# A two-layer decoder whose last mixture scatters its finished rows to the output and fetches its expert weights tile by tile

## The reference, cut to what matters

```
x = x + attn(LN(x)); x = x + xattn(LN(x), ctx); x = x + moe0(LN(x))        # layer 0: stages A, B, C
x = x + relattn(LN(x)); x = x + xattn(LN(x), ctx)                          # layer 1: stages D, E
h = x + attention(rms(x, g1));  out = h + moe1(rms(h, g2))                 # stages F, G

moe1(xf):                                                  # xf: 2048 tokens x 128
  vals, idx = top_k(xf @ router_w + router_b, 2);  scores = softmax(vals)
  emask = one_hot(idx) * (pos < cap);  tmask = sum(emask, -1);  m = max(assign, -1)
  y = (gelu((xf @ w2[m]) * (xf @ w1[m])) @ w3[m])          # one expert of 8 for each token, hidden 256
  out = sum_k scores[k] * (y if tmask[k] > 0 else xf)
```

## Time and profile before

| | us |
|---|---|
| median of 3 runs | 1674.38 |
| lowest, highest run | 1672.79, 1678.52 |
| profiled execution | 1675.38 |
| its span, first to last instruction | 1673.6 |
| mean granted TensorE clock (share of full) | 0.922 |

### The profile page before, as it was taken

One profiled execution on the slowest core, in us unless ns is written; L12 is line 12 of the kernel. 1 busy time (PEld: TensorE's weight loads), 2 busy tenths in 40 slices (PEclk: granted clock), 3 DMA queues, 4 the chain that ended last, 5 costly groups with the idle time before them and its releaser, 6 DMA issues.

```text
span 1673.6 us, 43831 instructions
## 1 busy us (share of the span) xinstructions
PE 1423.6 (85%) x17681; PEld 878.2 (52%) x17681; DVE 966.6 (58%) x2541; ACT 749.0 (45%) x1927; POOL 232.3 (14%) x201
## 2 busy tenths in 40 slices
PE   4889888696499999999958999889989898999672
PEld 3343434393266666766633466346644564456462
DVE  4354635323477777777723676576665776477532
ACT  1323142251266666666613276327723672447431
POOL 1011120123030030200010200030002100120124
PEclk7989999797799999999978899999989998899897
DMA  9600000023230100100021000000000000000012
GB/s 327 264 17 1 17 1 7 17 58 98 77 140 4 26 19 10 35 4 16 4 76 43 1 2 2 5 7 2 2 5 7 2 2 1 7 1 1 6 55 70
DMA packets 62072, 60.07 MB, mean 36 GB/s; under 512 B 27952, under 2 KB 47024, under 8 KB 60720
## 3 DMA queue, kind: packets, MB, share of 16 engines
q1 hardware_dynamic: 59536, 53.04, 10.0%
q0 software_dynamic: 2048, 4.20, 0.9%
q10 hardware_dynamic: 288, 0.03, 0.0%
HBM read 32.73 MB, written 24.51 MB: 34 GB/s over the span
## 4 chain that ended last, share of the span: by engine, by line
PE 69%; DVE 15%; issue 4%; SPq 4%; DMA 3%; ACT 3%; POOL 2%; ACTq 0%; POOLq 0%; DVEq 0%
PE ps L1126 7%; PE ps L1514 6%; PE ps L1533 5%; PE ps L500 5%; PE ps L1547 4%; PE ps L1106 4%; PE ps L1116 4%; DVE arena L586 4%; PE ps L1147 4%; PE ps L258 4%; PE ps L1502 3%; PE ps L474 3%; PE ps L1161 2%; PE ps L1556 2%; PE ps L797 2%
## 5 line engine op out<-in xcount | busy, mean ns | idle before, releaser
L1259 DVE TENSOR_REDUCE nmax<-ps 128x1 f32<-128x512 f32 x256 | 166.8, 683 | 56.3 <-PE ps L1116 55.7
L1590 ACT ACTIVATE arena<-ps,arena 128x512 f32<-128x512 f32 (+3 forms) x256 | 135.5, 531 | 119.1 <-DVE arena L1650 112.9
L1650 DVE TENSOR_REDUCE arena<-ps 128x1 f32<-128x512 f32 (+3 forms) x256 | 124.3, 487 | 78.8 <-PE ps L1518 76.7
L1219 ACT ACTIVATE arena<-ps,nmax 128x512 f32<-128x512 f32 x172 | 119.0, 692 | 80.8 <-DVE nmax L1259 79.3
L1533 PE MATMUL ps<-sqc,arena 128*128 128x128 f32 x640 | 106.6, 287 | 20.0 <-DVE arena L1658 19.7
L586 DVE TENSOR_REDUCE arena<-ps 128x8 f32<-128x1232 f32 x64 | 89.2, 1438 | 40.3 <-PE ps L462 40.1
L258 PE MATMUL ps<-identb 128*128 128x512 bf16 x408 | 110.0, 430 | 1.4 <-DVE kcol L707 1.4
L1267 DVE COPY arena<-ps 128x512 f32<-128x512 f32 x128 | 88.0, 688 | 39.9 <-PE ps L1126 38.4
L1514 PE MATMUL ps<-arena 64*128 64x384 f32 (+3 forms) x512 | 106.2, 493 | 0.0
L1658 DVE TENSOR_SCALAR arena<-arena 128x512 f32<-128x512 f32 (+3 forms) x256 | 100.8, 394 | 9.1
L598 DVE RECIPROCAL arena<-ps 128x128 f32<-128x128 f32 x8 | 7.7, 959 | 160.4 <-PE ps L500 160.4
(11 more groups left out here) (350 smaller groups left out, 2713.1 us busy)
## 6 DMA issues: line engine op xcount, KB each, us to landing
xs_d<-onehot SPq DMA_DIRECT2D x3, 3072.0 KB, 29.6
cw<-in_cw SPq DMA_DIRECT2D x2, 2048.0 KB, 13.4
rv<-in_rv SPq DMA_DIRECT2D x2, 1536.0 KB, 19.7
late<-in_gw SPq DMA_DIRECT2D x3, 1024.0 KB, 10.8
arena<-xs_d SPq DMA_DIRECT2D x46, 64.0 KB, 1.8
xs_d<-arena SPq DMA_DIRECT2D x46, 64.0 KB, 1.6
xs_d<-onehot SPq DMA_DIRECT2D x1, 2560.0 KB, 22.4
onehot<-q_s SPq DMA_DIRECT2D x96, 8.0 KB
```

What stands on the lines that cost most here:

```text
L1219: nc.scalar.activation(PB[k % 6], ps[:, k % 5, :], ACT.Exp, bias=nmax[:, u:u + 1], accum_out=rsum[:, b % 2, u:u + 1]).then_inc(SD["exp"], 1)
L1259: nc.vector.tensor_reduce(nmax[:, k % NU:k % NU + 1], ps[:, k % 5, :], AX.X, ALU.max, negate=True)\
L1590: nc.scalar.activation(TF["p%d" % (n % 2)][:, h * S:h * S + wd], ps[:, FSB[n % 2][h], 0:wd], ACT.Exp, bias=TF["nmax"][:, k4:k4 + 1], accum ...
L1650: nc.vector.tensor_reduce(TF["nmax"][:, k4:k4 + 1], ps[:, FSB[n % 2][h], 0:wd], AX.X, ALU.max, negate=True)\
```

## The change: what it does, and the diff

1. **Rows.** For G there is a new DRAM table `gs_d` of 23,552 rows of 258 floats (1032 bytes). A row holds the normed token, its residual, its weight `cy` and its token number less 4096. They lie in SBUF as `G4`, in the space of stage C's weights (`cw`). GpSimd scatters whole rows of it.
2. **Clearing.** `gs_d` is cleared by four DMAs of GpSimd (`pool_G_zero`), placed between `pool_C` and `pool_D`. The old `xs_d` and its clearing by SyncE stay, for stage C.
3. **Result.** VectorE's last step of a tile multiplies by the row's `cy` and adds the row's residual. GpSimd then scatters the 128 finished rows to `out`; rows with an index out of bounds (the cleared ones) are left out. The store to the table, the gather of 16 times 128 rows, the 16 adds and the output stores are gone.
4. **Weights.** w1 and w2 of G are no longer resident (group 4 loses two loads of 1 MB), and GpSimd doesn't copy them. SyncE reads the expert's number and issues two loads from DRAM per tile, into four buffers.
5. **Masks.** The eight mask steps, and the two copies of `cpick` and `cmask`, go from VectorE to GpSimd (`pool_prepare`), before GpSimd's first work for stage B. VectorE keeps the two small steps for `pcol`, now after the norm of stage B.
6. Three small VectorE instructions that write the token numbers, before D1.

```diff
+        def pool_prepare(pool):
+            pool.wait_ge(s_const[1], 16 * len(GROUPS[1]))
+            nc.gpsimd.tensor_copy(xmask[:, :, 0:KP], xmask_in)
+            nc.gpsimd.tensor_copy(xmask[:, :, KP:KW], xmask_in[:, :, 0:KW - KP])
+            for mask, given in ((amask, amask_in), (kmask, kmask_in)):
+                nc.gpsimd.memset(mask[:, :, KS:KP], MASKED)
+                nc.gpsimd.tensor_scalar(mask[:, :, 0:KS], given[:, :, :], MASKED, None, ALU.mult)
+                ins = nc.gpsimd.tensor_scalar(mask[:, :, KP:KW], given[:, :, 0:KW - KP], MASKED, None, ALU.mult)
+            ins.then_inc(s_mask, 1)
+            nc.gpsimd.tensor_copy(cpick[:, :, :], causal_in[:, 0:2, :])
+            nc.gpsimd.tensor_copy(cmask[:, :, :], causal_in[:, 2:4, :]).then_inc(s_mask, 1)
...
         def pool_G_send(pool, b):
             pool.wait_ge(SG["slot"], b + 1)
-            for n in range(NT):
-                nc.gpsimd.indirect_dma_start(xs_d, bass.IndirectOffsetOnAxis(ap=slot4[:, b * NT + n:b * NT + n + 1], axis=0),
-                                             yn4(b)[:, n, :], None).then_inc(SC["sent"], 16)
+            if b == 0:
+                pool.wait_ge(SG["zero"], 16 * 4)
+            for n in range(b * NT, b * NT + NT):
+                nc.gpsimd.indirect_dma_start(gs_d, bass.IndirectOffsetOnAxis(ap=slot4[:, n:n + 1], axis=0),
+                                             G4[:, n, :], None).then_inc(SC["sent"], 16)
...
                 if s >= 4:
-                    dve.wait_ge(SC_st[s % 4], 16 * (st_c[s % 4] + s // 4))
-                V.tensor_copy(TG[f"y{s % 4}"], ps[:, 6 + s % 2, 0:P]).then_inc(SC["yb"], 1)
-            for b in range(B):
-                dve.wait_ge(SC_yg[b], 2 * 16 * NT)
-                for i in range(NT):
-                    ins = V.scalar_tensor_tensor(xo4(b)[:, i, :], yg4(b)[:, i, :], cy4[:, b * NT + i:b * NT + i + 1], xo4(b)[:, i, :],
-                                                 ALU.mult, ALU.add)
-                ins.then_inc(s_xout, 1)
+                    dve.wait_ge(SG_out[s % 4], 16 * (s // 4))
+                V.scalar_tensor_tensor(TG[f"y{s % 4}"], ps[:, 6 + s % 2, 0:P], XBG[s % NXB][:, 2 * P:2 * P + 1],
+                                       XBG[s % NXB][:, P:2 * P], ALU.mult, ALU.add).then_inc(SC["yb"], 1)
 
         def sp_G(sp):
             sp.wait_ge(SC["sent"], 2 * 16 * NTT)
             sp.wait_ge(SG["table"], 1)
+            for s in range(NS):
                 r = sp.value_load(rows4[0:1, s:s + 1], min_val=0, max_val=XROWS - P)
                 if s >= NXB:
-                    sp.wait_ge(SC["tx"], NS + s - NXB + 1)
-                sp.dma_start(XBG[s % NXB], xs_d[bass.ds(r, P), :]).then_inc(SC_ld[s % NXB], 16)
+                    sp.wait_ge(SC["yb"], NS + s - NXB + 1)
+                    sp.wait_ge(SG["idx"], s - NXB + 1)
+                sp.dma_start(XBG[s % NXB], gs_d[bass.ds(r, P), :]).then_inc(SC_ld[s % NXB], 16)
+                e = sp.value_load(expert4[0:1, s:s + 1], min_val=0, max_val=E2 - 1)
+                if s >= NWB:
+                    sp.wait_ge(SC["h"], NS + s - NWB + 1)
+                for m, n in enumerate(("gw1", "gw2")):
+                    sp.dma_start(TG[f"w{s % NWB}"][:, m * HID2:(m + 1) * HID2],
+                                 t[n][:, bass.ds(e, 1), :].rearrange("p o n -> p (o n)")).then_inc(SC_st[s % NWB], 16)
+            for z in range(4):
+                sp.wait_ge(SG_out[z], 16 * st_c[z])
+
+        def pool_G_zero(pool):
+            zero = kmask[:, :, :].rearrange("p b n -> p (b n)").bitcast(F32)[:, 0:GW4]
+            nc.gpsimd.memset(zero, 0.0).then_inc(s_own, 1)
+            pool.wait_ge(s_own, 2)
+            rows = gs_d.rearrange("(p r) d -> p r d", p=P)
+            for z in range(4):
+                r0, r1 = z * XROWS // P // 4, (z + 1) * XROWS // P // 4
+                nc.gpsimd.dma_start(rows[:, r0:r1, :], zero.unsqueeze(1).to_broadcast([P, r1 - r0, GW4])).then_inc(SG["zero"], 16)
+
+        def pool_G(pool):
+            for s in range(NS):
+                pool.wait_ge(SC_ld[s % NXB], 16 * (ld_c[s % NXB] + s // NXB + 1))
+                if s >= 4:
+                    pool.wait_ge(SG_out[s % 4], 16 * (s // 4))
+                nc.gpsimd.tensor_scalar(gidx[:, s % 4:s % 4 + 1], XBG[s % NXB][:, 2 * P + 1:GW4], 2.0 * B * S, None, ALU.add)\
+                    .then_inc(SG["idx"], 1)
+                pool.wait_ge(SG["idx"], s + 1)
+                pool.wait_ge(SC["yb"], NS + s + 1)
+                nc.gpsimd.indirect_dma_start(out_rows, bass.IndirectOffsetOnAxis(ap=gidx[:, s % 4:s % 4 + 1], axis=0),
+                                             TG[f"y{s % 4}"], None, bounds_check=B * S - 1, oob_is_err=False)\
+                    .then_inc(SG_out[s % 4], 16)
...
             pool_C_send(pool, B - 1)
             pool_C(pool)
+            pool_G_zero(pool)
             pool_D(pool)
```

More of the change, by code:

```diff
@@ L707, in dve_masks @@
             nc.vector.tensor_copy(kcol[:, :, :].rearrange("p b j -> p (b j)"), ps[:, 1, 480:480 + B * NPER]).then_inc(s_flipped, 1)
+        def pool_prepare(pool):
[9 more added lines that the diff above has]
+            nc.gpsimd.tensor_copy(cmask[:, :, :], causal_in[:, 2:4, :]).then_inc(s_mask, 1)
         def dve_prepare(dve):
             dve.wait_ge(s_const[1], 16 * len(GROUPS[1]))
[L712 to L720, removed]
             nc.vector.tensor_reduce(pcol[:, :], vmask[:, :, :], AX.X, ALU.max).then_inc(s_prep, 1)
-            dve.wait_ge(s_prep, 5)
+            dve.wait_ge(s_prep, 4)
             nc.vector.tensor_scalar(pcol[:, :], pcol[:, :], 1.0, -MASKED, ALU.subtract, ALU.mult).then_inc(s_prep, 1)
@@ L1686, in pool_F @@
                     .then_inc(SF["qr"], 1)
-        SG = {n: sem("s_g_" + n) for n in ("gate", "d", "e2", "oh", "cum", "seen", "pick", "rank", "slot", "count", "table", "a", "p")}
+        SG = {n: sem("s_g_" + n) for n in ("gate", "d", "e2", "oh", "cum", "seen", "pick", "rank", "slot", "count", "table", "a", "p", "zero", "idx")}
+        SG_out = [sem("s_g_out%d" % i) for i in range(4)]
         ld_c, st_c = ([len(range(z, NS, n)) for z in range(n)] for n in (NXB, 4))
@@ L1949, in pool_G @@
-        def pool_G(pool):
-            pool.wait_ge(SG["table"], 1)
-            for s in range(NS):
-                e = nc.gpsimd.value_load(expert4[0:1, s:s + 1], min_val=0, max_val=E2 - 1)
-                if s >= 2:
-                    pool.wait_ge(SC["h"], NS + s - 1)
-                nc.gpsimd.tensor_copy(TG[f"w{s % 2}"].rearrange("p (m n) -> p m n", m=2),
-                                      gw12[:, :, bass.ds(e, 1), :].rearrange("p m o n -> p m (o n)")).then_inc(SC["w1"], 1)
-            for z in range(4):
-                pool.wait_ge(SC_st[z], 16 * 2 * st_c[z])
-            for n in range(NTT):
-                nc.gpsimd.indirect_dma_start(yg4(n // NT)[:, n % NT, :], None, xs_d,
-                                             bass.IndirectOffsetOnAxis(ap=slot4[:, n:n + 1], axis=0)).then_inc(SC_yg[n // NT], 16)
+                    sp.wait_ge(SC["yb"], NS + s - NXB + 1)
@@ L2045, in _ @@
             sp_G(sp)
-            for b in range(B):
-                sp.wait_ge(s_xout, b + 1)
-                sp.dma_start(out[b:b + 1].rearrange("o (t p) d -> p (o t) d", p=P), xo4(b)).then_inc(s_store, 16)
-            sp.wait_ge(s_store, B * 16)
         @block.tensor
@@ L2135, in _ @@
             ch.turn(0)
+            ch(nc.vector.tensor_reduce(g_p[:, 0:1], c["tri"], AX.X, ALU.add))
+            ch(nc.vector.tensor_scalar(g_p[:, 0:1], g_p[:, 0:1], -1.0, float(P - 2 * B * S), ALU.mult, ALU.add))
+            ch(nc.vector.tensor_scalar(G4[:, :, 2 * P + 1], row["index"][:, 0:NTT], float(P), g_p[:, 0:1], ALU.mult, ALU.add))
             for b in range(B):
```

58 lines of the change are left out of this document (29 added, 29 removed).

## The result

The changed kernel takes 1754.96 us (median of 4 runs, 1753.42 to 1756.55), the kernel before 1676.45 (4 runs): a ratio of 1.0468, 95% interval 1.0439 to 1.0497. Forecast was 1666, range 1652 to 1695. The profiled execution took 1754.84 us, its span is 1753.0, which is 79.4 us more than before.

What follows compares the result with a forecast made beforehand. TensorE was taken to carry most stages (69% of the chain), SyncE to pace G's loop. 1673.6 - 4.6 (masks) + 8 (clearing in D0) - 11.9 (G) = 1665.1 of span, a median of 1666; range 1652 to 1695.

Steps and rivals of the forecast that it cites:

- the clearing's share of D0: Rest of stage D0: GpSimd's clearing DMAs delay SyncE's stores and loads there, costing 8 us.
- the upper bound: D0: each SyncE packet waits for one clearing packet, 64 x 118 ns a sequence, 22.6 us for three.
- the right rival: Clearing collides with D0 in full: 22.6 us in place of 8, median 1680; chance 0.15.
- The rival of the late GpSimd: D's second sequence: clearing at the indirect DMA price frees GpSimd late, stall 48 us, median 1709; chance 0.22.
- The forecast of "nothing" here: D's second sequence: GpSimd, busy 100 us with the clearing, is free in time for its preparation, costing nothing.
- The masks: Stage A, first sequence: masks on GpSimd let VectorE's line 386 start at 18.9, not 23.56, saving 4.6 us.
- The loop and the end of G: Stage G: a tile every 2.72 us at SyncE's pace, end about 3 us after the last result, saving 11.9 us.
- The third DMA: Loop of G: SyncE's added DMA per tile, without a number read from SBUF, costs 0.5 us (0.34 to 0.76).
- the rival of a heavier SyncE: Loop of G: third DMA also costs 1.11 us, a tile takes 3.33 us, median near 1680; chance 0.06.

Runs made afterwards that it cites:

- run 1: Kernel before plus only the new table and its clearing by four GpSimd DMAs between stages C and D, nothing reading it: 1753.29 us, ratio 1.0462.
- run 3: Kernel before plus the same 24.3 MB cleared from GpSimd's queue in pieces of 2048 bytes in place of 1032: 1728.1 us, ratio 1.0312.
- run 4: Changed kernel with the clearing issued by SyncE in stage B, in quarters, in place of GpSimd after stage C: 1666.63 us, ratio 0.9936.
- run 7: Kernel before plus a quarter of the table cleared from ScalarE's hardware queue, behind its last D0 step for the first sequence: 1690.18 us, ratio 1.0088.

## Why the prediction was wrong

*The failed step is the clearing's share of D0.* I took 8 us, with 22.6 as the upper bound; it was 96.9 (83.3 with the clearing alone). That the clearing would lie on D0's stores and loads, and that turns between packets set the price, was right. Three sizes in it were off.

**The packet's length.** I divided the time of GpSimd's queue by its 2048 packets and took 118 ns for a packet of 2 KB. But these packets are of two kinds. In the DMA view of the kernel before, 395 to 401, where only gathers run, 74 of 154 packets are under 512 bytes:

```profile
q0 software_dynamic: 154, 0.33, 20.7%
```

The other 80 hold 4.1 KB and take some 248 ns each (0.207 x 16 x 6 / 80). With this the bound of 64 packets and three sequences would have been 48 us. The clearing's own packets held four rows of 1032 bytes and took 272 ns alone and 303 ns in the changed kernel, 68 to 76 ns a row. The earlier trace rows gave 410 GB/s for pieces of 2 KB, and I carried this rate over to rows of half the length; so the transfer lasted 120 to 136 us and not 59 to 88.

**What lies on the path.** I counted three sequences of 64 packets an engine, 192, but the reloads of x, k and v for D and the last sequence are there too, some 264 packets (4 times 32 stored, 3.5 times 32 small loads, 24 in reloads).

**The turns.** One for one was no upper bound, because a small load costs two. As an estimate from these counts, 264 packets at one turn of 303 ns are 80 us, and with a second turn for the 112 small loads 114; the measured 96.9 lies between. With the 272 ns of run 1 it is 72 to 102, and 83.3 was measured.

The Trainium skill's rule on turns (page "DMA: Bandwidth & Descriptors", section "Queues, rings and completion order": whole packets, one queue after the other) pointed at the right rival, and I gave it 0.15 and a wrong price. The runs agree with it, one packet for one, where 2 KB packets are served (550 to 550 in run 3); beside small loads they show two for one. The Trainium skill's formula for a GpSimd DMA (same page, section "Anatomy of one DMA — SWDGE (gpsimd) path") gave 64 us as an estimate for the four together; 136 were measured.

*The rival of the late GpSimd fell.* A clearing DMA of 5888 rows took GpSimd 2.2 us to issue, not 46 times 0.947. It did stand 64.85 us before the third (for want of room in the queue, it seems; no run shows it), and was free at 472; line 1357 ran from 562.95, when its data was there, and no one waited for it. The forecast of "nothing" here was right, for a reason of its own.

*The masks* were right in place and sign: I had 4.6 us, line 346 started 4.4 us earlier (21.00 against 25.42), and with the clock back at full sooner it was 6.7 us at the end of stage C in the first profile, and 7 by the ratio when alone. GpSimd's mask steps were slower than both rows that I used (1.84 us for 616 columns from int32), the signal came at 25.9 and not by 23.7, but stage A covered it, as the text had it.

*The loop and the end of G* were right in mechanism and off in size. A tile takes 2.68 us where nothing stalls (1729.50 to 1732.18), forecast 2.72; with stalls the 22 steps took 61.4 us, a mean of 2.79, and from the first load to the last weights' issue it was 63.6 us, 2.0 more than my 61.6 (1591.5 to 1653.1). The last weights to the last result took 6.3 us in place of 5.6. From the last result to the end I had 3.0 us, which was 6.9: the last three results come 1.4 us apart, GpSimd needs 2.12 for each, so the last scatter is issued 2.3 us late, and it ends 4.6 us after its issue. These 2.0, 0.7 and 3.9 us are the 6.6 that were missing of the 11.9. The third DMA, taken at 0.5 us, was 0.43, but it was worth more than its issue: without it G is 12 us shorter. So the rival of a heavier SyncE, 3.33 us a tile, fell. TensorE's granted clock over the loop (1678 to 1738) was 0.91, where it was 0.96 before.

## What to carry to other kernels

A large transfer in the background is not free because no engine waits for it. Ask which small DMAs with someone waiting behind them lie beside it, and count all their packets, for a packet of 128 bytes waits as long as one of 2 KB, or longer. Price each at one packet of the large transfer, and the small loads at two. Take a packet's length from rows that hold one kind of packet alone; an average over two kinds gave half of it here. Put the transfer where the DMA engines are idle (here stage B) and cut it in pieces of 2 KB, not in the rows' odd length. Do not carry a rate over from pieces of another length.

## What was not expected of the hardware

- Rows of 1032 bytes went at 197 to 266 GB/s with full DMA engines from GpSimd's queue (the change and run 1) and at 216 from SyncE's (run 4, 120 to 150 us); the same bytes in pieces of 2048 at 374 to 388. A piece costs 68 and 86 ns.
- GpSimd's queue put four rows of 1032 bytes in a packet (5888 packets for 23,552 rows), the hardware queues one (5888 for the quarter's 5888 rows in run 7).
- The kernel before spread over 1660 to 1684 us in 28 runs, more than the 0.3% that I took. The profiles show TensorE's granted clock falling at other moments in stages A and B: line 258 of the first sequence takes 3.19 us in one execution and 6.16 in another, and a sequence 71.7 or 74.8 us.
- In the profile of the clearing alone, D's first product came 83.3 us later and the end 77.5, so 5.8 came back in between. In the window from 357 to 557 us after D's first product, TensorE's granted clock was 0.95 where it was 0.91 before.
